# A two-layer graph network with experts: the first tiles of the second aggregation, their waits and what stands between them

## The reference

```python
xn = layernorm(x)
agg1 = segment_sum(xn[src], dst) / deg
h = relu(xn @ W0_0 + b0_0 + agg1 @ W1_0 + b1_0)                 # 512 wide
agg2 = segment_sum(h[src], dst) / deg
x2 = x + (h @ W0_1 + b0_1 + agg2 @ W1_1 + b1_1) + mix(xn)       # linear attention
xf = layernorm(x2)
top_v, top_i = top_k(xf @ Wg + bg + bias, 2)
combine = (one_hot(top_i, 8) * softmax(top_v)[..., None]).sum(1)
y = einsum(relu(einsum(xf, W1) + b1), W2) + b2                  # (rows, expert, 256)
out = x2 + einsum(y, combine)
```

## Time and profile before

| what | us |
|---|---|
| median of 3 runs | 2245.94 (2245.6 to 2248.06) |
| the profiled execution | 2241.64, span 2240.1 |
| PE busy | 2075.8 (93% of the span) |
| DVE / ACT / POOL busy | 1551.8 / 1198.9 / 369.5 |
| products of the second aggregation and the first (L2272), 4753 | 1149.1 |
| hidden layer ends on PE, tile 0 starts | 1316.7, 1321.3 |
| mean DMA rate | 134 GB/s |

### The profile page before, as it was taken

One profiled execution on the slowest core, in us unless ns is written; L12 is line 12 of the kernel. 1 busy time (PEld: TensorE's weight loads), 2 busy tenths in 40 slices (PEclk: granted clock), 3 DMA queues, 4 the chain that ended last, 5 costly groups with the idle time before them and its releaser, 6 DMA issues.

```text
span 2240.1 us, 52353 instructions
## 1 busy us (share of the span) xinstructions
PE 2075.8 (93%) x15356; PEld 1310.5 (59%) x15357; DVE 1551.8 (69%) x4887; ACT 1198.9 (54%) x2466; POOL 369.5 (16%) x438
## 2 busy tenths in 40 slices
PE   3887888999999999999999988999999995999997
PEld 2676675555565555555454544444444443899996
DVE  6898987999999999999645544455555444455554
ACT  3677663555555555555656543444444443566664
POOL 2000000000000000000111111111111222466665
PEclk9999998999999999999999999999999997999998
DMA  3333227222222222222534336555555554565552
GB/s 94 90 89 96 81 96 210 116 116 113 111 114 116 116 116 114 110 111 116 179 132 166 111 115 227 194 194 200 199 201 198 192 194 162 138 97 92 90 92 43
DMA packets 158735, 299.12 MB, mean 134 GB/s; under 512 B 31774, under 2 KB 107855, under 8 KB 156419
## 3 DMA queue, kind: packets, MB, share of 16 engines
q1 hardware_dynamic: 131075, 243.66, 31.3%
q0 software_dynamic: 25856, 47.15, 9.3%
q10 hardware_dynamic: 1664, 6.35, 0.8%
HBM read 148.32 MB, written 144.19 MB: 131 GB/s over the span
## 4 chain that ended last, share of the span: by engine, by line
PE 68%; issue 13%; DVE 8%; DVEq 4%; DMA 2%; POOLq 2%; POOL 1%; ACT 1%; ACTq 0%; SPq 0%
PE bank L2272 44%; PE bank L2263 6%; PE bank L2513 6%; PE bank L2498 6%; DVEq L1166 2%; POOLq L843 1%; DVE big L1123 1%; DVE big L1136 1%; PE bank L2480 1%; DVEq L1132 1%; DVE big L1118 1%; PE bank L2280 1%; DVE big L1134 1%; DMA big<-rows_dram 1%; PE bank L2141 1%
## 5 line engine op out<-in xcount | busy, mean ns | idle before, releaser
L2272 PE MATMUL bank<-RW,big 128*128 128x512 f16 x4753 | 1149.1, 380 | 0.0
L2272 PEld LDWEIGHTS bank<-RW,big 128*128 128x128 f16 x4753 | 431.6, 98 | 385.0 <-issue 3.6
L1920 ACT ACTIVATE big<-bank 128x512 f16<-128x512 f32 (+1 forms) x640 | 364.2, 573 | 316.5 <-PE bank L2263 316.4
L1294 DVE TENSOR_TENSOR big<-iotaB,keys 128x512 f16<-128x512 f16 x1300 | 451.9, 417 | 7.9 <-issue 6.8
L2263 PEld LDWEIGHTS bank<-big 128*128 128x128 f16 x2560 | 190.9, 98 | 106.2 <-issue 1.4
L2263 PE MATMUL bank<-big 128*128 128x128 f16 x2560 | 247.5, 219 | 0.4 <-issue 0.4
L977 POOL DMA_INDIRECT out_dram<-big x112 | 179.9, 1606 | 110.1 <-ACT big L2066 74.7
L910 POOL DMA_DIRECT2D big<-in_L_ffn_W_dram x8 | 6.2, 778 | 1052.5 <-DVE R L1353 1051.7
L2057 ACT ACTIVATE big<-bank,b1A,iscA 128x256 f32<-128x256 f32 x224 | 114.2, 560 | 98.2 <-PE bank L2498 93.6
L2513 PE MATMUL bank<-RW,big 128*128 (+1 forms) x1344 | 157.7, 274 | 0.4 <-DVE big L1717 0.3
L2498 PE MATMUL bank<-big,RW 128*128 128x256 f16 x1344 | 156.3, 273 | 0.4 <-ACT big L2046 0.4
(11 more groups left out here) (421 smaller groups left out, 2925.4 us busy)
## 6 DMA issues: line engine op xcount, KB each, us to landing
big<-a_dram SPq DMA_DIRECT2D x48, 800.0 KB, 6.0
big<-a_dram SPq DMA_DIRECT2D x48, 768.0 KB, 4.3
a_dram<-big SPq DMA_DIRECT2D x49, 640.0 KB, 2.9
a_dram<-big SPq DMA_DIRECT2D x49, 512.0 KB, 2.6
a_dram<-big SPq DMA_DIRECT2D x49, 416.0 KB, 2.4
big<-rows_dram SPq DMA_DIRECT2D x56, 265.0 KB
big<-in_x_dram SPq DMA_DIRECT2D x96, 128.0 KB, 2.1
own_dram<-big SPq DMA_DIRECT2D x48, 256.0 KB, 2.5
```

What stands on the lines that cost most here:

```text
L1294: last = v.tensor_tensor(out[q].rearrange("p b (m k) -> p b m k", k=2), inturn(iotaB[:, :], QB, P // 2), twice(kd[:, q * QB:(q + 1) * QB, ...
L1920: a.activation(Ab[q][:, 0:n], banks[BB(q)][:, 0:n], ACT.Copy).then_inc(s_ab, 1)
L2272: last = mm(bank[:, :], blk(q, c), R2[:, u * 2 * D:(u + 1) * 2 * D], start=(i == 0), stop=(i == T - 1))
```

## The change

Five things move; nothing is computed in another way.

- On PE, tile 0 waits at its start only for sources up to tile 41 and for bank 5, and then before blocks 42 to 47 and before the last one for each one's own source (`s_yl`). The product of the gate bias goes from in front of tile 0 to behind it.
- On DVE the copy of the gate bias no longer has a signal of its own; `scales(7)` moves from behind tile 0 to behind tile 1, both `lows(7, j)` to behind tile 2.
- On ACT `norms(7)` and `highs(7, 0)` move behind tile 1's copy, `highs(7, 1)` behind tile 2's.
- On POOL `expert` is cut in two, `drawn` (loads and the sum) and `kept` (the store). They follow each other as before, only that for the eighth expert the waits for the end of the hidden layer and the branch for overflowing rows stand between them.
- On SP the load of `b2` to all partitions goes from behind tile 1's small loads to behind the loop.

```diff
--- before.py
+++ after.py
@@ -723,10 +723,6 @@
                 sp.dma_start(io["out"][bass.ds((t - 1) * P, P), :], R3[:, bass.ds((t - 1) * D, D)]).then_inc(s_x2, 16)
 
             rows_x(1)
-            sp.wait_ge(s_wst, 16 * EXPERTS)
-            sp.dma_start(b2b.rearrange("p e n -> p (e n)"),
-                         io["L0_ffn_b2"].rearrange("(a e) n -> a (e n)", a=1).to_broadcast([P, EXPERTS * D]))\
-              .then_inc(s_b2, 16)
             load_a(3, 1, 2)
             rows_x(2)
             with sp.Fori(1, T // 2 - 1) as k:
@@ -734,6 +730,10 @@
                     t = 2 * k + i + 1
                     load_a(t + 1, i, t)
                     rows_x(t)
+            sp.wait_ge(s_wst, 16 * EXPERTS)
+            sp.dma_start(b2b.rearrange("p e n -> p (e n)"),
+                         io["L0_ffn_b2"].rearrange("(a e) n -> a (e n)", a=1).to_broadcast([P, EXPERTS * D]))\
+              .then_inc(s_b2, 16)
             load_a(T - 1, 0, T - 2)
             rows_x(T - 2)
             sp.wait_ge(s_xrf, T)
@@ -902,7 +902,7 @@
             for i in range(3):
                 pool.wait_ge(s_st[i], 16 * T + 16)
 
-            def expert(e, first):
+            def drawn(e, first=False):
                 if first:
                     w1s, w2s, b1s = (io[f"L0_ffn_{n}"][0:1] for n in ("W1", "W2", "b1"))
                 else:
@@ -916,18 +916,24 @@
                 if not first:
                     wait(s_wst, e * 16)
                 nc.gpsimd.partition_all_reduce(nr3, sq3, P, RADD).then_inc(s_wr, 1)
+
+            def kept(e, first=False):
                 wait(s_wh, 2 * e + 2)
                 wait(s_wo, e + 1)
                 dst = w_dram[0, :, :] if first else w_dram[bass.ds(e, 1), :, :].rearrange("a p c -> (a p) c")
                 pool.dma_start(dst, wout).then_inc(s_wst, 16)
 
-            expert(0, True)
-            with pool.Fori(1, EXPERTS) as e:
-                expert(e, False)
+            drawn(0, True)
+            kept(0, True)
+            with pool.Fori(1, EXPERTS - 1) as e:
+                drawn(e)
+                kept(e)
+            drawn(EXPERTS - 1)
             pool.wait_ge(s_yl, 1 + T)
             pool.wait_ge(s_zc, 3 + T)
             with pool.If(lacking > 0):
                 overflow(1)
+            kept(EXPERTS - 1)
 
             def weights(e):
                 if e:
@@ -1661,13 +1667,13 @@
             v.tensor_copy(gpart[:, :, 2, :], gres2[:, :, :]).then_inc(s_gs, 1)
 
 
-            dve.wait_ge(s_gp, 1)
-            v.tensor_copy(gb, banks[0][:, 0:8]).then_inc(s_gv, 1)
             dve.wait_ge(s_yp, W + T)
             dve.wait_ge(s_yl, 1 + T)
             dve.drain()
             with dve.If(lacking > 0):
                 overflow(1, rd2)
+            dve.wait_ge(s_gp, 1)
+            v.tensor_copy(gb, banks[0][:, 0:8])
 
             v.memset(seen, 0.0)
 
@@ -1686,11 +1692,11 @@
                 finish2(t)
 
             iterate2(0, None, None)
+            iterate2(1, (0, 0), None)
             scales(EXPERTS - 1)
+            iterate2(2, (1, 1), (0, 0))
             for j in range(2):
                 lows(EXPERTS - 1, j)
-            iterate2(1, (0, 0), None)
-            iterate2(2, (1, 1), (0, 0))
             with dve.Fori(1, T // 2) as k:
                 iterate2(2 * k + 1, (2 * k, 0), (2 * k - 1, 1))
                 iterate2(2 * k + 2, (2 * k + 1, 1), (2 * k, 0))
@@ -1958,17 +1964,16 @@
                     for q in range(LEAD):
                         evac(0, q)
                 iterate(L, 0, None, banks[5])
-                if L == 1:
-                    norms(EXPERTS - 1)
-                    for j in range(2):
-                        highs(EXPERTS - 1, j)
                 if L == 0:
                     with act.Fori(0, T // 2) as k:
                         iterate(0, 2 * k + 1, None, banks[7])
                         iterate(0, 2 * k + 2, None, banks[5])
                 else:
                     iterate(1, 1, (0, 0, None), banks[7])
+                    norms(EXPERTS - 1)
+                    highs(EXPERTS - 1, 0)
                     iterate(1, 2, (1, 1, None), banks[5])
+                    highs(EXPERTS - 1, 1)
                     with act.Fori(1, T // 2) as k:
                         iterate(1, 2 * k + 1, (2 * k, 0, k), banks[7])
                         iterate(1, 2 * k + 2, (2 * k + 1, 1, k), banks[5])
@@ -2357,9 +2362,9 @@
                         pe.wait_ge(s_A[0][0], 16)
                     if i == 6 * QB:
                         pe.wait_ge(s_A[0][1], 48)
-                    if i == 0:
-                        pe.wait_ge(s_yl, 1 + T)
                     u = 0 if i == T - 1 else T - 1 if i == 0 else i
+                    if i == 1 or u >= T - W:
+                        pe.wait_ge(s_yl, 2 + max(u, T - W - 1))
                     last = mm(bank[:, :], first_blk(q, c), R2[:, u * 2 * D:(u + 1) * 2 * D], start=(i == 1), stop=(i == 0))
                 last.then_inc(s_ap[1], 1)
 
@@ -2384,9 +2389,11 @@
 
             def tiles2():
                 tile0(banks[5])
+                pe.wait_ge(s_gv, 1)
+                pe.wait_ge(s_ha, 8 * (T // W) + 4)
+                mm(banks[0][:, 0:8], ones[0:1, :], grows[0:1, 2, :], start=True, stop=True).then_inc(s_gp, 1)
                 pe.wait_ge(s_zc, 3 + T)
                 pe.wait_ge(s_gs, 1)
-                pe.wait_ge(s_gv, 2)
                 tile2(1, 1, 0, (0, 0), None, banks[7])
                 tile2(2, 0, 1, (1, 1), (0, 0), banks[5])
                 for k in range(1, T // 2):
@@ -2449,16 +2456,12 @@
             hidden(T // W - 1, 0, 16 * (T // W // 2 + 1))
 
 
-            pe.wait_ge(s_gv, 1)
-            pe.wait_ge(s_ha, 8 * (T // W) + 4)
-            mm(banks[0][:, 0:8], ones[0:1, :], grows[0:1, 2, :], start=True, stop=True).then_inc(s_gp, 1)
             with pe.If(lacking > 0):
                 pe.wait_ge(s_yl, 1 + T)
                 pe.wait_ge(s_zc, 3 + T)
-                pe.wait_ge(s_gv, 2)
+                pe.wait_ge(s_ha, 8 * (T // W) + 4)
                 overflow(1)
-            pe.wait_ge(s_yl, T)
-            pe.wait_ge(s_zc, T + 1)
+            pe.wait_ge(s_zc, 3 + T - W + max(i for i in range(W) if Y4(i) == 5) + 1)
             tiles2()
             before2(T - 2, 1)
             transposed2(T - 1, 0)
```

## The result

| kernel | median, us | runs | against before |
|---|---|---|---|
| before | 2245.60 (2241.86 to 2248.95) | 9 | |
| after | 2253.72 (2248.79 to 2255.75) | 9 | ratio 1.0036, interval 1.0026 to 1.0046 |

The change costs 8.1 us; the prediction said 2255.3 and slower. In the profiled executions the spans differ by 13.0 us (2253.1 and 2240.1). Of these, 3.03 lie ahead of the passage: PE's last product group of the hidden layer starts at 1318.66 for 1315.63 of before, in code that the change doesn't touch. **From here on, "corrected" means a time of the trace after less 3.03.** The profiled spans differ by another 1.4 us behind the passage, which isn't traced further.

What follows compares the result with a forecast made beforehand. PE bounds the kernel, with three holes, the last ended by POOL's chain from expert 7's store. Gains of 10.8 are eaten; +6.8 (transposes) and +2.6 (clock) make +9.4: 2255.3 us from the median 2245.94, range 2250 to 2262.

Steps and rivals of the forecast that it cites:

- Part 1: Tile 0's early start: PE gains 6 us, but the copy waits for ACT's squares, so only -0.8 us is left.
- Part 2: Scales out of tile 0: row tile 0's transposes at 1337.9 against 1347.17, PE standing 3.3 us without clock fall.
- Part 3: Scales behind tile 1: row tile 1's transposes at 1349.95 after a 1.1 us stand, PE 10.8 us ahead of before.
- Part 4, the store: POOL's store of expert 7 behind tile 2's low halves, 1.4 us after their end: at 1361.0, 12.9 us later.
- Part 4, the chain: Store to row tile 2's transposes: 26.7 us less 4.8 (second reload) and 1.4 (scatter), 20.5; transposes at 1381.5, +6.8.
- Slow clock: PE runs slow for a while after standing over 20 us in tile 3: +2.6 us.
- b2 behind the loop: b2's 1 MB load after the loop, wanted two tiles later: costs nothing; without that cover up to 4.9 us.
- Sum: At the end of tile 3: lead of 10.8 eaten whole, +6.8 and +2.6 make +9.4 us.
- (1): Expert 1's load and scatter don't shrink, clock also falls in tile 1: +6.2 + 2.6 more; 0.17 including what lies between.
- (2): POOL's drain was not for the transfer: transposes 15.5 us after the store, +4.4, 2250.3; chance 0.10.
- (3): Row tile 2 doesn't wait for POOL, PE keeps its lead: transposes 13.5 us earlier, 2232.4; chance 0.08.
- (4): Tile 0's early start is used up by the squares: in the sum already; parts 2 to 4 alone, +0.8; no chance given.

Runs made afterwards that it cites:

- experiment 1: Kernel before with only tile 0's early start and the gate bias product behind it: 2245.08 us, -0.3 against before (0.9998).
- experiment 7: Kernel after with POOL's order changed: scatters 0 and 1, store, scatter 2, reload 0, scatter 3, reload 1: 2240.69 us, -4.7 against before.
- experiment 4: Kernel after with scatters 0 and 1 out of the loop, without helper and drain, still behind both reloads: 2248.15 us, +3.2 against before.
- experiment 2: Kernel after with b2's load put back behind tile 2's small loads, tile 4's matrix load queued behind it: 2257.77 us, +12.4 against before.
- experiment 5: Kernel after with POOL's order store, scatters 0 to 2, reload 0, scatter 3, reload 1; drains left out: 2239.96 us, -5.0 against before.
- 8: Kernel of experiment 7 plus one tiny unused addition on POOL ahead of the first scatter: 2231.07 us, -13.9 against before (0.9938).
- experiment 6: Kernel after with ACT's copy of tile 0's bank ahead of the eighth expert's squares: 2246.75 us, +1.8 against before (1.0009).
- experiment 9: Kernel of 8 with tile 0's copy also ahead of the eighth expert's squares: 2227.62 us, -18.6 against before (0.9921).
- 10: Kernel of experiment 9 with tile 0 again waiting for all sources and the gate bias: 2231.69 us, -14.5 against before (0.9940).
- 11: Kernel before with scatters 0 to 2 between store and reload 0, scatter 3 between reloads, without drains: 2241.69 us, -4.5 against before.
- experiment 3: Kernel after with the second high half and both low halves one tile earlier, behind tile 1: 2245.92 us, +0.5 against before (1.0003).

## Why the prediction was right, point by point

All times of after are corrected. The mechanism held at every link; some sizes did not, and the exact time of the store is luck.

- **Part 1** holds. Tile 0 from 1316.5 to 1327.2 (predicted 1316.9 to 1327.5), the copy at 1333.04 (1333.0), and the gain of 6 us on PE ended at the squares; experiment 1 gives -0.3 for the -0.8.
- **Part 2**: the transposes of row tile 0 at 1337.92 (1337.9) after a wait of 3.36 (3.3). The choice "no fall of the clock" was wrong: the granted clock was 0.53 over the 3.2 us behind it and tile 1's copy came 5.85 us after the transposes, not 4.2. The price was +1.65, less than the +2.6 kept for the range. It might have been that: in experiment 7, with the same code up to there, PE waited 3.66 and tile 1's copy came 6.87 after the transposes, +2.7.
- **Part 3**: transposes of row tile 1 at 1351.31 (1349.95), after 0.62 (1.1). The 1.36 are what was left of that fall.
- **Part 4, the store**: at 1361.00 (1361.0), by luck: two errors cancel. The low halves ended at 1360.8 instead of 1359.6, the same lateness handed on; the store came 0.2 us behind them instead of 1.4. The term of 1.4 was taken between 0.85 and 2.4, and the 2.4 had another cause than a neighbour's traffic: in before, POOL stood 7.14 us between its sum and its next addition (its row stands at experiment 7), and that ended later than DVE's halves. After, the first addition has been made at 1357.24, in a wait of 17.42, and nothing is left of the stand. The shared interfaces that the prediction weighed (Trainium skill, GPSIMD Engine Reference, section 1) would have given 1.0 more. The trace agrees with the rule itself: POOL's tiny addition takes 1.28 us beside DVE's low half of the seventh expert (1316.71 and 1316.66 in before) and 0.47 beside a DVE addition of 0.42 (that of 1357.24), for 0.19 in most places. But the addition in front of this store waits for just those halves, so it starts when they are through, and takes 0.19.
- **Part 4, the chain**: 19.8 (20.5). The second reload landed in 5.3 (5.4 taken, 10.2 before), the scatter in 2.95 (2.7 taken, 4.12 before), and 0.8 came from the first reload, which I had held at no change: the issue of the second followed the store in 8.05 instead of 8.87. Of that, 0.5 is the branch for overflowing rows, which before had between store and first reload and after has ahead of the store. Experiment 4 shows the drain as the transfer's, and experiment 2 that b2's place, with the matrix load behind it, is 3.4 of the 4.9. An estimate by the Trainium skill's page DMA: Bandwidth & Descriptors (Anatomy of one DMA) gives 4.4 for such a transfer; the trace has 5.3 here and 4.9 at best.
- **Slow clock** behind the long wait: 2.57 (2.6). PE stood 18.36 us ("over 20").
- **b2 behind the loop** cost nothing that shows: PE's longest wait in the experts' stage is 12.6 after and 12.5 before.
- **Sum**: +8.6 in the trace (9.4), +8.1 in the medians.
- **Rivals.** (1) Nothing shrinks: excluded by 5.3 and 2.95. (2) The drain not for the transfer: excluded by experiment 4, which had to take the drain away to reach its 15.5. (3) Row tile 2 doesn't wait for POOL: not so in this order, but experiments 5, 7 and 8 build it. The rival said 13.5 below before; the full order gave only 4.7 in experiment 7, and 13.9 once the stand of POOL was out of its way. These orders also left out the drain, so that 13.9 lies near 13.5 proves nothing. (4) Tile 0's gain eaten by the squares: experiment 6 takes the squares away and gets 6.3 us, of which the fall of the clock is a part.

What stays open: what POOL does in its stand, of which the rows show only the pair that opens it; why it was 9.21 in experiment 7 and 10.30 in 9; and whether the third scatter's 9.25 us in experiment 7 were due to the store, the reload or the matrix load. Beside a store a scatter landed in 3.01 (experiment 5), beside a reload in 4.31 (experiment 4), beside a matrix load in 6.45 (experiment 9), so none of them alone has given 9.25.

## What to carry to other kernels

A step that is moved later takes along everything that its engine has queued behind it: here six small steps moved by one or two tiles to spare PE a wait of 6.59 us, and a store, two reloads and the first scatters went with them. So ask of each move which in-order queue waits for the moved result, follow that queue to its last customer, and put transfers whose result is wanted late (reloads for the next stage) behind those that someone waits for now. A drain counts as a customer too: it holds the queue until the engine's own last transfer has landed (4.9 us in experiment 4). A gain upstream counts only if each link behind it is moved too; tile 0's early start was worth 0 or 4 us with the same edit.

## What the runs showed of the hardware

- **POOL stands before the first addition that follows a sum over partitions**: 6.8 to 7.4 us with nothing to wait for (7.14 before, 7.18 in experiment 1, 6.82 in 8, 6.85 in 10, 7.44 in 11), 9.21 in 7 and 10.30 in 9; and 5.5 to 6.7 ahead of the sum itself. It belongs to the change of instruction, since a dummy addition takes it. Transfers beside it don't explain the two long ones: DMA moved 260 GB/s during the 6.85, and 193 and 175 during the 9.21 and the 10.30. The Trainium skill states (GPSIMD Engine Reference, section 2.1) that the first call of a freshly loaded routine pays about 6 us for loading its code, with no instruction to be seen. The trace agrees in kind; here it is paid at each switch between the two kinds, not once.
- **POOL's tiny addition slows down beside DVE**: 1.28 us beside a DVE operation of 1.28 with two inputs and 0.47 beside one of 0.42, for 0.19 as its median.
- **PE's clock** fell to half after the wait of 3.36 us and not after the 2.93 us of before; in the other traces it fell after each wait of 3.39 or more and not after 2.82, 2.47 and 2.27 (experiments 3, 1 and 9). The price of a fall is not told by the wait: 1.65 after 3.36, 2.7 after 3.66 (experiment 7), 2.6 after 4.98 (5), 1.5 after 5.68 (11), 2.6 after 6.59 and after 18.36.
- **One megabyte on POOL's queue** took 5.3 us to land with no other large load beside it, 7.1 beside the end of a matrix load (experiment 3), and 8.7 (experiment 2) and 10.2 (before) beside both b2 and a matrix. A drain behind it in that queue lasts as long.
